# Folding the setup and the scatter-table program into the first attention's prologue

## The reference

```python
x = x + tanh(g_xattn[0]) * L0_xattn(layernorm(x), ctx)   # 32 heads of 16, axial rope, keys from ctx
x = x + tanh(g_ffn[0])   * L0_ffn(layernorm(x))          # 16 experts, top 4, and a shared one
x = x + tanh(g_xattn[1]) * L1_xattn(layernorm(x), ctx)
x = x + tanh(g_ffn[1])   * L1_ffn(layernorm(x))
# L1_ffn(x):
deltas   = softmax(expert_atom_weights) @ atoms           # (8, 4096)
weighted = deltas * sigmoid(importance)
rows, cols = mask_idx // 512, mask_idx % 512              # 4096 places in a 512 x 512 map
vals     = einsum('tk,tks->ts', rw, weighted[top_idx])    # rw: softmax of the two largest gate logits
contrib  = segment_sum((x[:, cols] * vals).T, rows)
out      = x @ W.T + contrib.T
```

## Time and profile before

| | us |
|---|---|
| median of 3 runs | 2080.91 (2078.62 to 2081.79) |
| the profiled execution | 2078.01 |
| its span | 2076.2 |
| last result of the scatter program (DVE) | 49.2 |
| first instruction of the attention program | 55.5 |
| first scores on PE | 92.7 |
| last work of the attention program | 643.7 |
| first instruction of the stage after it | 646.0 |

### The profile page before, as it was taken

How to read it: one execution, slowest core, us unless ns; L and a number is a source line. 1 busy time by engine, 2 the same in 40 slices (tenths; PEclk the granted TensorE clock), 3 DMA queues, 4 the chain that set the end, 5 groups by cost and what they waited for, 6 DMA issues and landing times. The chain is left out here.

```text
span 2076.2 us, 38678 instructions
## 1 busy us (share of the span) xinstructions
PE 1843.8 (89%) x11487; PEld 1407.4 (68%) x11487; DVE 1178.7 (57%) x2618; ACT 928.4 (45%) x2627; POOL 962.2 (46%) x1012
## 2 busy tenths in 40 slices
PE   4599999999986999999999999995689999886992
PEld 1355665666554999999999999993356566555881
DVE  5566677767653776433333343334777777764445
ACT  4267676767652332233333333321366666641110
POOL 1487777876741066133433334332455555311660
PEclk9899999999987999999999999998899999996996
DMA  8578877787755426589999988544345454529657
GB/s 324 183 233 271 255 224 249 248 261 229 224 159 171 155 63 206 165 248 269 296 319 280 281 247 248 114 77 112 83 94 117 105 115 101 131 94 374 233 163 273
DMA packets 233756, 414.81 MB, mean 200 GB/s; under 512 B 44289, under 2 KB 121225, under 8 KB 228242
## 3 DMA queue, kind: packets, MB, share of 16 engines
q1 hardware_dynamic: 167194, 324.12, 49.0%
q0 software_dynamic: 30592, 62.54, 13.1%
q10 hardware_dynamic: 35776, 25.69, 4.0%
HBM read 211.97 MB, written 157.82 MB: 178 GB/s over the span
## 5 line engine op out<-in xcount | busy, mean ns | idle before, releaser
L705 ACT ACTIVATE a_P<-a_SC,a_nm 128x256 f32<-128x256 f32 x512 | 235.9, 473 | 130.4 <-DVE a_nm L607 129.6
L1227 POOL DMA_INDIRECT b_y_rows<-b_ysb,b_entry x79 | 124.4, 1575 | 334.6 <-ACT b_ysb L1375 182.2
L607 DVE TENSOR_REDUCE a_nm<-a_SC 128x2 f32<-128x512 f32 x256 | 164.8, 685 | 142.2 <-PE a_SC L838 142.2
L570 POOL TENSOR_TENSOR a_praw<-a_praw,a_phigh 128x704 f32<-128x704 f32 (+2 forms) x126 | 191.8, 1523 | 10.3
L1479 DVE TENSOR_TENSOR b_xl<-b_XT,b_xh 128x512 fp32r<-128x512 f32 x97 | 67.1, 692 | 216.8 <-ACT b_xh L1381 216.3
L849 PEld LDWEIGHTS a_T<-ident,a_P 128*128 128x128 f32 x1024 | 118.5, 144 | 79.6 <-issue 46.3
L849 PE MATMUL a_T<-ident,a_P 128*128 128x128 f32 x1024 | 145.3, 280 | 20.9 <-DVE a_PT L619 17.8
L568 POOL CAST a_phigh<-a_praw 128x704 fp32r<-128x704 f32 (+2 forms) x126 | 111.3, 883 | 100.2 <-DMA a_praw<-in_L_ffn_wd 34.2
L2212 ACT ACTIVATE c_P<-c_SC,c_nm 128x240 f32<-128x240 f32 x256 | 115.7, 457 | 75.8 <-DVE c_P L2084 75.8
L1485 DVE TENSOR_TENSOR b_al<-b_AT,b_ah 128x384 fp32r<-128x384 f32 x111 | 61.9, 558 | 150.0 <-ACT b_ah L1386 150.0
L1375 ACT ACTIVATE b_ysb<-b_Y 128x512 f32<-128x512 f32 x79 | 47.2, 598 | 222.2 <-PE b_Y L1322 212.3
(11 more groups left out here) (494 smaller groups left out, 4923.6 us busy)
## 6 DMA issues: line engine op xcount, KB each, us to landing
w_parts<-a_phigh SPq DMA_DIRECT2D x72, 352.0 KB, 3.7
w_parts<-a_praw SPq DMA_DIRECT2D x72, 352.0 KB, 4.1
b_wh<-w_parts SPq DMA_DIRECT2D x18, 1216.0 KB, 10.3
b_wl<-w_parts SPq DMA_DIRECT2D x18, 1216.0 KB, 13.8
c_q<-c_qT SPq DMA_DIRECT2D x64, 256.0 KB, 4.2
c_k<-c_kT SPq DMA_DIRECT2D x124, 128.0 KB
b_wh<-w_parts SPq DMA_DIRECT2D x18, 704.0 KB, 4.7
b_wl<-w_parts SPq DMA_DIRECT2D x18, 704.0 KB, 7.3
```

The costliest lines, as they stand in the source:

```text
L570: eng.tensor_tensor(raw[:, 0:k * m], raw[:, 0:k * m], r32(high[:, 0:k * m]), ALU.subtract).then_inc(plow_done, 1)
L607: eng.tensor_reduce(nm[:, g % 4, j, :], SC[j][:, :].rearrange("p (t k) -> p t k", t=BT), AX.X, ALU.max, negate=True).then_inc(topped, 1)
L705: e = eng.activation(Pr[:, i, t, :], SC[j][:, t * S:(t + 1) * S], ACT.Exp, bias=nm[:, g % 4, j, t:t + 1], accum_out=den[:, h, t:t + 1])
L1227: eng.indirect_dma_start(out=y_rows, out_offset=bass.IndirectOffsetOnAxis(ap=entry[:, r, 1:2].bitcast(U32), axis=0), in_=ysb[:, v % RING, ...
```

## The change

`setup` and `scatter_tables` are gone as blocks; their work is put into `rope_attention`, so that two ends of blocks go. In new line numbers:

- SP loads the first sequence's tokens second (512 KB), then the weights; the gates' loads stand behind them. W goes to `Wraw`, the tokens of sequences 2 to 7 are loaded in slot -7, and the broadcast indices (`row_i`, 2 MB) in slot -2, once two of the buffers are out.
- The first sequence has tables of its own (`FIRST_ITEMS_AT` and others). PE turns all of W in slot -12 into the banks of the scores and of the turned exponentials.
- ACT widens in eight halves (128 x 2048) in slots -12 to -3, into five buffers; the 6th, 7th and 8th reuse buffers 3, 4 and 2 and wait until those are written out. SP writes two halves in slot -9, three in slot -8, behind the first exchange, and three in slot -3.
- The layer-norm scalars of sequence 0 are made first, those of sequence 1 in slot -6, and those of the other twelve tiles in slots 0 to 10.
- The weighted values are made turned: items E0 and E1 on PE (32 small products in place of 16 wide ones and 32 transposes), `place_weights` on DVE in slot -3. `match` (eight pieces of 128 x 512) is on DVE in slots 3 to 6, `earlier` on POOL in slots 4 to 7, items S0 and S1 on PE in slots 6 and 8, `place_half` on DVE in slots 7 and 9.
- The pieces of the weight split begin in slot 12 instead of -6, with a second piece in every slot 16n + 13, and end in slot 129 instead of 119. The indirect DMAs of the first sequence are in slots 10 to 16.

The core of the diff:

```diff
-    COLUMN_AT = {3: 0, 7: 1, 11: 2, 15: 3}
-    SPLIT_AT, NRAW, NHIGH = -6, 4, 3
+    FIRST_ITEMS_AT = {-15: ("X0", "X1"), -14: ("Q0",), -13: ("K0",), -12: ("Q1",), -11: ("q0a",), -10: ("K1",),
+                      -9: ("V0", "k0a"), -8: ("q1a",), -7: ("V1",), -6: ("q0b", "k0b"), -5: ("q1b",), -4: ("E0", "E1"),
+                      -3: ("k1a",), -2: ("k1b",), 6: ("S0",), 8: ("S1",), ...}
+    FIRST_ROTATE_AT = {-14: 0, -13: 1, -12: 2, -10: 3}
+    FIRST_COLUMN_AT = {10: 0, 12: 1, 14: 2, 16: 3}
+    SPLIT_AT, NRAW, NHIGH = 12, 4, 3
+    WIDEN_AT = {-12: 0, -11: 1, -10: 2, -9: 3, -8: 4, -6: 5, -5: 6, -3: 7}
+    SEND_AT = {-9: (0, 1), -8: (2, 3, 4), -3: (5, 6, 7)}
+    KEPT_IN = (0, 1, 2, 3, 4, 3, 4, 2)
...
# SP
+            eng.dma_start(ea[:, 0, :], eaw).then_inc(ea_in, 16)
+            eng.dma_start(core.X[:, 0:BT, :], xf[:, 0:BT, :]).then_inc(x_in[0], 16)
...
+            def late_loads(s):
+                for h in SEND_AT.get(s, ()):
+                    send_wide(h)
+                if s == -7:
+                    for i in range(3):
...
+                if s == -2:
+                    for i in (3, 4):
+                        eng.wait_ge(wide_out[i], WIDE_OUT[i])
+                    eng.dma_start(row_i[:, :, :].rearrange("p c q -> p (c q)"), mask_idx.partition_broadcast(P)).then_inc(rows_in, 16)
...
+                if s == SPLIT_AT - 2:
+                    eng.wait_ge(placed, 1)
# ACT
+            def widen(h):
+                k, part, i = h // 2, slice(RH * (h % 2), RH * (h % 2 + 1)), KEPT_IN[h]
+                eng.wait_ge(maps_turned, k + 1)
+                if KEPT_IN.index(i) < h:
+                    eng.wait_ge(wide_out[i], 16)
+                eng.activation(wide[i][:, :, :], map_bank[k][:, part].unsqueeze(2).to_broadcast([P, RH, E]),
+                               ACT.Copy).then_inc(wide_ready, 1)
...
+            eng.wait_ge(graw_in, 32)
+            eng.activation(core.gates[:, :], graw[:, :], ACT.Tanh).then_inc(gates_set, 1)
             for s in range(FIRST, LAST):
...
+                if s == -15:
+                    sines(eng)
# PE
+                if s == -12:
+                    eng.wait_ge(W_in, 16)
+                    for k in range(KD):
+                        turn_maps(k)
+                if s == -2:
+                    eng.wait_ge(wide_ready, 4)
+                if s == 0:
+                    eng.wait_ge(wide_ready, 8)
# DVE
+                if s == -11:
+                    addresses()
+                if s == -3:
+                    place_weights()
...
+                if s == -6:
+                    second_stats()
...
+                later_stats(s)
+                for j in range(MATCHES * (s - MATCH_AT), MATCHES * (s - MATCH_AT + 1)):
+                    if 0 <= j < C // MATCH:
+                        match(j)
```

More of the change, by code:

```diff
@@ L310, in rope_tables, with rope_attention @@
     return load, angles, sines, tables
-def rope_attention(nc, core, ctx_d, pos, Wq, Wkv, Wout, bout, gate, add_column, columns_added, split):
+def rope_attention(nc, core, x, ctx_d, pos, Wq, Wkv, Wout, bout, g_xattn, g_ffn, placing, table, split):
     H, HD = 32, 16
@@ L365, in items, with split_before, due @@
         return [(b, n) for b, n, i, j in pieces(s) if j == TERMS.get(n[0], 1)]
-    def due(s, table):
-        return [(b, table[s - PAIRS * b]) for b in range(B) if s - PAIRS * b in table]
+    def split_before(s):
+        return min(max(0, s - SPLIT_AT) + sum(n % PAIRS == SPLIT_TWO for n in range(SPLIT_AT, s)), split.count)
+    def due(s, first, others):
+        return [(b, at[s - PAIRS * b]) for b, at in ((b, others if b else first) for b in range(B)) if s - PAIRS * b in at]
     number = {}
@@ new lines, in _, with send_wide @@
+            for i in range(2):
+                eng.dma_start(at_[A * i:A * (i + 1), :], atoms[:, NS // 2 * i:NS // 2 * (i + 1)]).then_inc(atoms_in, 16)
+            def send_wide(h):
+                k, part, i = h // 2, slice(RH * (h % 2), RH * (h % 2 + 1)), KEPT_IN[h]
+                eng.wait_ge(wide_ready, h + 1)
+                eng.dma_start(table[k * P * D:(k + 1) * P * D, :].rearrange("(p r) e -> p r e", p=P)[:, part, :],
+                              wide[i][:, :, :]).then_inc(wide_out[i], 16)
@@ new lines, in second_stats, with later_stats @@
+            def second_stats():
+                eng.wait_ge(x_in[1], 16)
+                layer_norm_scales(eng, vseq, c, core.X, core.st, llw, lnsc, slice(BT, 2 * BT))
+                eng.wait_ge(vseq, c.now)
+                eng.sem_inc(all_scales, 1)
+            def later_stats(s):
+                if s in range(0, NT // 2 - 2):
+                    t = 2 * s + 4
+                    eng.wait_ge(x_in[t // 4 + 1], 16)
+                    for t in (t, t + 1):
+                        eng.bn_stats(core.st[:, t, :], core.X[:, t, :]).then_inc(vseq, c.inc())
+                if s == 6:
+                    eng.wait_ge(vseq, c.now)
+                if 6 <= s < 11:
+                    for _ in range(5):
+                        next(later_scalars, None)
+                if s == 10:
+                    assert next(later_scalars, None) is None
+                    eng.wait_ge(vseq, c.now)
+                    eng.sem_inc(all_scales, 1)
```

532 lines of the change are left out of this document (290 added, 242 removed).

## The result

The changed kernel took 2108.6 us (median of four runs, 2104.94 to 2123.71) against 2079.8 for the kernel before, a ratio of 1.016 (95% interval 1.010 to 1.021). It is 29 us slower, where 2057 was predicted in a range of 2042 to 2072, with 0.06 for slower. The profiled execution took 2110.35 us, span 2108.5; before, 2078.01 and 2076.2.

What follows compares the result with a forecast made beforehand. Prediction: two serial programs, DMA-bound table writes and a chain of small steps, fill 93 us before the first scores. Terms -36 + 12.3 + 0.5 = -23.2 us gave a forecast of 2057 us, range 2042 to 2072.

Steps and rivals of the forecast that it cites:

- First exponential: Prologue: first exponential on ACT at 58.6 us instead of 94.6, a gain of 36 us.
- its bounds: Prologue: first exponential between 51 us (44 us gained) and 66 us (28 us gained).
- The gates' load: Start of prologue: gates land at 17 us behind 4.25 MB, holding ACT's tanh and the tokens' copy; 12 to 14 if they overtake.
- The first rotation: Prologue: DVE's first rotation starts at about 22 us, after the tokens' copy, sines and tables.
- everything issued from about 0.8 us: Start of prologue: all loads taken as issued from about 0.8 us, the basis for their landing times.
- Slots 0 to 11: First attention slots: added DVE work costs 10.3 us and POOL's selects 2, together 12.3 us; bounds 6 and 27.
- The last summand: In slots 0 to 11, what is left to slot 10: 9.7 busy and 4.1 added in 12.8 us, costing 1.3 us.
- The clock rival: Slots 3 to 10: DVE-bound slots keep PE at its lower clock, 27 us more, total 2072; chance 0.13.
- From slot 12 on nothing in the change alters what PE does: Attention loop from slot 12: no cost, so only the earlier first exponential, slots 0 to 11 and the end count.
- The split rival: Weight split: POOL's pace of 4.17 us a piece makes 126 late pieces outlast the attention, 35 us lost, 2092; chance 0.06.
- POOL had room in slots with a piece: Argument against the split's being slower: POOL was 2.2 us busy of 3.55 in slot 3.
- The end: Attention's end: last split piece in slot 129, some 6 us before the end with 4 us of landing; cost 0.5 us.

Runs made afterwards that it cites:

- e5: e3 with the gates' tanh moved on ACT from the start to slot -6, ahead of the sixth widening: 2056.5 us.
- e1: Kernel before with only the split's schedule changed: pieces from slot 12, second piece in every slot 16n + 13: 2126.4 us.
- e7: e1 with five raw and four high buffers in place of four and three: 2084.4 us.
- e9: e1 with four high buffers in place of three, raw buffers still four: 2126.2 us.
- e13: e1 with five raw buffers in place of four, high buffers still three: 2083.0 us.
- e3: Changed kernel with the second piece of each sequence in slot 16n + 9 instead of 16n + 13: 2060.6 us.
- e14: Changed kernel, second piece still at 16n + 13, with five raw buffers in place of four (sines' buffers laid over aT): 2067.7 us.
- e10: e5 with a small exponential in slot -6 to load its table early, and the third table write ahead of the exchange: 2052.6 us.
- e15: e10 with five raw buffers: 2049.5 us.

## Why the prediction was wrong

- **First exponential.** -36 predicted, -31.7 measured, inside its bounds. The mechanism was right: the tanh holds ACT, the widenings wait for the writes behind the exchange. The gates' load landed at 19.65 us, not 17, and the tanh was all that held the tokens: in e5 their copy moves to 11.95. The first rotation came at 26.84 instead of 22, and the difference lies ahead of it: from there to the first exponential it took 36.1 us where 36.6 had been worked out. The working had "everything issued from about 0.8 us"; SP issued the loads one behind the other, and the gates' only at 9.80 us. The Trainium skill (DMA: Bandwidth & Descriptors, Queues, rings and completion order) says that each DMA engine takes its ring's descriptors in order; the trace agrees: issued at 9.80 us behind 4.25 MB the load took 9.8 us to land, and 2.6 us alone.
- **Slots 0 to 11.** From the first exponential on, +12.3 predicted and +8.9 measured. Two errors met in it. I left out what the removed pieces give back there: 5.1 to 7.2 us in the four kernels with the late split (e1, e7, e9, e13). The added work then costs about 14 to 16 by these numbers, not 12, so that +8.9 below the forecast is luck in part. The last summand was misadded too: 9.7 and 4.1 in 12.8 us are 1.0 over, not 1.3. Part of the cost is the clock. PE's 40.3 us in slots 3 to 10, at a mean 0.82, were 33.7 at 0.95, with some 2 us of added work among them. The clock rival's mechanism was there at about 5 us of PE's busy time, not at the 27 of its price; how much of it reached the total time is not shown.
- **From slot 12 on.** "From slot 12 on nothing in the change alters what PE does" is the step that failed. The change moves 126 pieces and puts two in every sixteenth slot, and I costed that edit by its end alone (0.5 us). What I did not do is count the ring: load two slots ahead, write-out one slot behind, four buffers. That is a sum of the text of the code, and it leaves a landing of 3.4 to 3.9 us one slot of 3.5 us and more with one piece a slot, and none behind a slot with two. Measured: 51.5 us lost from slot 12 to slot 127, of which the one number of e3 gives back all and the fifth raw buffer of e14 42.6.
- **The split rival** named the right part at 0.06 and the wrong mechanism: a pace of POOL of more than 3.9 us a piece, with the attention waiting at its end. The attention did not wait for POOL at its end: the last piece was done at 666.4 us, 7 us ahead of the attention's last work. What was late is the other work in POOL's and SP's order, behind the pieces. "POOL had room in slots with a piece", said against it, was true of POOL's time and did not bear on the question, because the wait is SP's.
- **The end.** 0.5 us was right for the changed kernel itself (19.1 us from slot 127 to the next stage against 18.5), by luck: the term counted the last landing, and what the late pieces cost is DVE's scalars and then the clock. In e3, e5, e10, e14 and e15 it is 3.1 to 4.9 us.
- With the one number of the second piece set to 9, the time is 2060.6, 17 us under the kernel before; the forecast was 23 under. That this is near is luck in part: in e3 the first exponential is 4.9 us later than worked out and the end 4.4 us longer, while slots 0 to 11 cost 4.7 us less and the later slots gain 2.5.

## What to carry to other kernels

When a schedule puts a second item into a slot, count each ring by slots: how many slots ahead is the load issued, how many behind the write-out, and what is left of the ring for a landing. Where nothing is left, the engine that issues waits, and with it everything behind it in its order, here an exchange and the write-outs that POOL needed; the wait's sum tells little (150.9 us of waiting with the second piece at 16n + 9, 111.1 in the kernel that is 48 us slower), its place between the things that others wait for tells all. And the releaser that the waiting engine names can be one step from the cause: make that buffer deeper alone, and see whether the time moves.

## What the runs showed of the hardware

- A stall of PE costs more than its length: 3.3 us of waiting in slot 16n + 1 made the interval 6.3 us longer, since the 55 matmuls behind it took 7.37 us instead of 4.36 with a granted clock of 0.68 (0.50 for the first 4.4 us).
- A load of 1 KB that was issued at 9.80 us behind 4.25 MB on the same queue took 9.8 us to land; alone it took 2.6.
- Moved out of the tokens' way, the tanh between two widenings took 0.20 us and needed no table load of its own behind the sigmoid; an exponential taken early put its table load of 1.28 us into ACT's wait for a write.
- A DVE instruction of 128 x 14 values took 0.17 us in the kernel before, where POOL had no pieces left, and up to 1.14 in e3 beside POOL's subtraction of 128 x 512 values; the twenty of them took 3.5 us there and 8.3 in e3.
